# DLRM tower: one-hot lookups in steps of 512 columns over two alternating groups of five tables, in place of steps of 256 columns for a pair of tables

## The reference

```python
e = jnp.stack([tbl_f[ids[:, f]] for f in range(26)], axis=1)        # 2048 x 26 x 128
combined = jnp.concatenate([e, r_dense_x[:, None, :]], axis=1)      # 27 vectors a sample
z = jnp.einsum('bfd,bgd->bfg', combined, combined)[:, TRIU_I, TRIU_J]   # 351 pairs
h = jnp.concatenate([z, r_dense_x], axis=1)                         # 479
h = jnp.maximum(h @ W_top1 + b_top1, 0.0)                           # 512
h = jnp.maximum(h @ W_top2 + b_top2, 0.0)                           # 256
y = h @ W_top3                                                      # 2048 x 1
```

## Time and profile before

| | |
|---|---|
| three runs, us | 373.93 median, 371.11, 374.20 |
| profiled execution, us | 374.13 |
| its span, us | 371.9 |
| PE, PEld busy, us | 345.5, 317.1 |
| DVE, ACT, POOL busy, us | 170.1, 184.4, 258.8 |
| mean granted clock | 0.986 |
| moved by DMA | 37.14 MB, mean 100 GB/s |

### The profile page before, as it was taken

One profiled execution on the slowest core, in us unless ns is written; L12 is line 12 of the kernel. 1 busy time (PEld: TensorE's weight loads), 2 busy tenths in 40 slices (PEclk: granted clock), 3 DMA queues, 4 the chain that ended last, 5 costly groups with the idle time before them and its releaser, 6 DMA issues.

```text
span 371.9 us, 13580 instructions
## 1 busy us (share of the span) xinstructions
PE 345.5 (93%) x6176; PEld 317.1 (85%) x6176; DVE 170.1 (46%) x380; ACT 184.4 (50%) x235; POOL 258.8 (70%) x265
## 2 busy tenths in 40 slices
PE   1998787989998999999999999999999999999997
PEld 0898776879897889999899998999899998899887
DVE  4589654533533435356245535356244635350220
ACT  3588242764345543473716643473725734376433
POOL 6688877777777777777777777777777777774000
PEclk9999899999998999999999999999999999999999
DMA  7967743211622126221262226321262222221000
GB/s 242 356 183 243 232 149 107 67 51 51 196 70 67 51 58 183 78 65 51 68 198 53 65 54 173 91 67 53 51 206 60 64 53 65 55 56 37 19 4 3
DMA packets 15917, 37.14 MB, mean 100 GB/s; under 512 B 5141, under 2 KB 7829, under 8 KB 15860
## 3 DMA queue, kind: packets, MB, share of 16 engines
q0 software_dynamic: 8192, 16.79, 16.9%
q1 hardware_dynamic: 7668, 19.48, 16.1%
HBM read 36.24 MB, written 0.01 MB: 97 GB/s over the span
## 4 chain that ended last, share of the span: by engine, by line
PE 69%; POOL 20%; issue 7%; DMA 3%; SPq 0%; ACT 0%
PE ps_lk L509 29%; POOL rows L242 20%; PE ps_gram L536 10%; PE ps_tr L521 6%; PE ps_zt L562 6%; PE ps_mlp L562 6%; PE ps_mlp L569 3%; PE ps_zt L569 3%; DMA zt<-in_tbl 2%; PE ps_mlp L577 1%; PE ps_lk L590 1%; PE ps_lk L489 1%; PE ps_zt L549 1%; DMA rows<-in_tbl,gather_ids 1%; PE ps_lk L597 0%
## 5 line engine op out<-in xcount | busy, mean ns | idle before, releaser
L242 POOL DMA_INDIRECT rows<-in_tbl,gather_ids x256 | 257.4, 1006 | 80.4 <-issue 76.2
L279 DVE TENSOR_SCALAR onehot<-ids_from 128x512 fp32r<-128x512 f32 x320 | 126.3, 446 | 94.1 <-PE ps_lk L509 68.7
L509 PE MATMUL ps_lk<-onehot,table 128*128 128x256 f32 x1248 | 163.3, 290 | 2.6 <-DVE onehot L279 2.0
L509 PEld LDWEIGHTS ps_lk<-onehot,table 128*128 128x128 f32 x1248 | 155.9, 196 | 4.3 <-issue 3.1
L360 ACT COPY xt<-ps_tr 128x512 f32<-128x512 f32 x64 | 77.0, 1203 | 93.0 <-PE ps_tr L521 91.2
L536 PEld LDWEIGHTS ps_gram<-xt 128*26 128x26 f32 x4096 | 44.1, 103 | 23.4 <-issue 20.7
L536 PE MATMUL ps_gram<-xt 128*26 128x26 f32 x4096 | 52.7, 192 | 9.8 <-issue 4.8
L350 ACT COPY xt<-ps_lk 128x512 f32<-128x512 f32 x40 | 48.9, 1236 | 14.5 <-PE ps_gram L536 10.5
L287 DVE STREAM_TRANSPOSE zs<-ps_gram 128x832 f32<-128x832 f32 x16 | 16.8, 1050 | 85.9 <-PE ps_gram L536 85.9
L521 PE MATMUL ps_tr<-ident,rows 128*128 128x128 f32 x256 | 39.3, 276 | 3.3 <-ACT xt L360 1.8
L521 PEld LDWEIGHTS ps_tr<-ident,rows 128*128 128x128 f32 x256 | 29.6, 140 | 7.1 <-ACT xt L360 2.4
(11 more groups left out here) (57 smaller groups left out, 153.7 us busy)
## 6 DMA issues: line engine op xcount, KB each, us to landing
ids<-in_ids_onehot SPq DMA_DIRECT2D x8, 768.0 KB
w<-in_tbl SPq DMA_DIRECT2D x8, 512.0 KB, 5.0
rows<-in_tbl,gather_ids POOLq DMA_INDIRECT x256
ids<-in_ids_onehot SPq DMA_DIRECT2D x7, 512.0 KB
dense_x<-in_dense SPq DMA_DIRECT2D x8, 128.0 KB
zt<-in_dense SPq DMA_DIRECT2D x8, 128.0 KB
ids<-in_ids_onehot SPq DMA_DIRECT2D x2, 256.0 KB, 4.1
h<-in_tbl SPq DMA_DIRECT2D x1, 512.0 KB, 5.9
```

The source lines that it names most:

```text
L242: pool.indirect_dma_start(rows[n % ROW_BUFS][:, r, :], None, t_[f"tbl_{GATHERED[r]}"], bass.IndirectOffsetOnAxis(ap=gather_ids[:, n, r:r + ...
L279: nc.vector.tensor_scalar(onehot[:, u % RING, :, :], ids_from[:, 2 * i:2 * i + 2, :], float(k), None, ALU.is_equal).then_inc(s_unit, 1)
L509: m = nc.tensor.matmul(bank(c, i)[:, j, :], table[:, 2 * i + j, part, k, :], onehot[:, u % RING, j, :], start=(k == 0 and j == 0 and part ...
```

## The change

- **Steps.** A list `STEPS` of (first chunk, tiles, tables) takes the place of the pairs. From chunk 1 on the ten tables are two fives, `FIRST` (0 to 4) and `SECOND` (5 to 9). A wide step does one table for four tiles: 8 slices x 2 parts = 16 products of 512 columns. Chunks 1, 3 and 5 start wide steps of `FIRST` for themselves and the next chunk, chunks 2, 4 and 6 of `SECOND`. Narrow steps (one or two tables for one chunk) remain: six in chunk 0, three of `SECOND` in chunk 1, three of `FIRST` in chunk 7. That is 42 steps for 40, 30 of them wide.
- **First step.** `lookup_first` does table 0 alone in full floats: 8 products for 16.
- **Planes.** DVE compares the raw int32 ids with a per-partition scalar `own[:, k]`. ACT's shifts, `ids_from` and its waits are gone. Ids come by step, 512 columns to a buffer, four buffers.
- **Buffers.** `xt` holds four tiles instead of two; row buffers go from three to two; raw tables are staged in four buffers that rotate instead of three.
- **Order.** POOL's `LEAD` counts change; its rule from `b` = 5 on is the same. In chunk 1 PE does three more lookups before layer 1; in chunk 7 none is left. DVE makes the fourth step of chunk 1 and the following ones after `pack(1)`. The tail turns the last group of the last tile later, behind both halves of layer 2 of chunk 6 and half of layer 1 of tile 14, and does tile 14's layer 2 before tile 15's layer 1.

```diff
-CT = 2
-CHUNKS = TILES // CT
-CS = CT * P
...
+CT = 2
+CS = CT * P
+CHUNKS = TILES // CT
+XT = 2 * CT
+N = XT * P
+HALF = NO // 2
+FIRST, SECOND = list(range(HALF)), list(range(HALF, NO))
+def by_chunk(tables, first):
+    cuts = [tables[:first]] + [tables[i:i + 2] for i in range(first, len(tables), 2)]
+    return [tuple(b) for b in cuts if b]
+STEPS = []
+STEP0 = []
+for c in range(CHUNKS):
+    STEP0.append(len(STEPS))
+    if c == 0:
+        STEPS += [(c, CT, b) for b in by_chunk(FIRST + SECOND, 1)]
+    elif c == CHUNKS - 1:
+        STEPS += [(c, CT, b) for b in by_chunk(FIRST, 0)]
+    else:
+        STEPS += [(c, XT, (i,)) for i in (FIRST if c % 2 else SECOND)]
+        if c == 1:
+            STEPS += [(c, CT, b) for b in by_chunk(SECOND, 0)]
+STEP0.append(len(STEPS))
+assert CHUNKS % 2 == 0 and TILES % XT == 0
...
-ROW_BUFS = 3
+ROW_BUFS = 2
...
+IDS = 4
-LEAD = (0, 2, 8, 14, 20)
-SPLIT = list(range(2, NO)) + [0, 1]
+LEAD = (0, 2, 6, 12, 20)
+SPLIT = list(range(1, NO)) + [0]
...
+        xt = sb("xt", [P, N, NF])
+        ids = [sb(f"ids{b}", [P, N], I32) for b in range(IDS)]
+        onehot = sb("onehot", [P, RING, N], F32R)
+        own_i = sb("own_i", [P, KT], I32)
+        own = sb("own", [P, KT])
...
+        RAWS = len(stage) - 1
+        raw = [stage[0] if j == 0 else stage[1 + SPLIT.index(j) % RAWS] for j in range(NO)]
+        ps_lk = [pb(f"ps_lk{i}", [P, N]) for i in range(LB)]
+        ps_tr = pb("ps_tr", [P, GROUP * P])
...
+        def slot(n):
+            a = n % XT * P
+            return slice(a, a + P)
...
+            def load_ids(e):
+                if e >= IDS:
+                    sp.wait_ge(s_unit, (e - IDS + 1) * KT)
                     sp.sem_inc(s_carrier["sp"], 1)
+                sp.dma_start(ids[e % IDS][:, :], t_["ids_onehot"][e:e + 1, :].to_broadcast([P, N])
+                             ).then_inc(s_ids[e % IDS], 16)
...
             def load_raw(j):
+                n = SPLIT.index(j)
+                if j > 0 and n >= RAWS:
+                    sp.wait_ge(s_low, n - RAWS + 1)
...
+            load_ids(0)
+            load_raw(0)
+            load_raw(1)
+            load_raw(2)
+            load_ids(1)
+            load_raw(3)
+            load_raw(4)
+            load_ids(2)
+            load_ids(3)
+            load_ids(4)
+            load_raw(5)
+            load_raw(6)
+            load_ids(5)
+            load_raw(7)
+            load_raw(8)
             load_dense_x(0)
+            load_ids(6)
+            load_raw(9)
             sp.dma_start(cols[:, :], t_["cols"]).then_inc(s_cols, 16)
+            for e in range(7, 10):
+                load_ids(e)
             sp.wait_ge(s_low, NO)
+            sp.sem_inc(s_carrier["sp"], 1)
             load_dense_z(0)
             load_dense_x(1)
+            for e in range(10, STEP0[2]):
+                load_ids(e)
...
+                    for e in range(STEP0[c + 1], STEP0[c + 2]):
+                        load_ids(e)
...
-                        pool.wait_ge(s_gpart, max(b - 2 * PARTS, 0) + 1)
+                        pool.wait_ge(s_gpart, b - 2 * PARTS + 1)
...
+            def make_units(e):
+                dve.wait_ge(s_ids[e % IDS], (e // IDS + 1) * 16)
+                for k in range(KT):
+                    if k % USE == 0 and e > 0:
+                        dve.wait_ge(s_unit_used, ((e - 1) * KT + k) // USE + 1)
+                    w = STEPS[e][1] * P * len(STEPS[e][2])
+                    nc.vector.tensor_scalar(onehot[:, k, 0:w], ids[e % IDS][:, 0:w], own[:, k:k + 1], None, ALU.is_equal
+                                            ).then_inc(s_unit, 1)
...
+            make_units(0)
+            for e in range(1, STEP0[1]):
+                for n in range(len(STEPS[e][2])):
+                    low(STEPS[e][2][n] - 1)
+                make_units(e)
             low(NO - 1)
             dve.wait_ge(s_const, 3)
+            dve.sem_inc(s_carrier["dve"], 1)
+            make_units(STEP0[1])
+            pack(0)
+            make_units(STEP0[1] + 1)
+            make_units(STEP0[1] + 2)
+            pack(1)
+            for i in range(3, 7):
+                make_units(STEP0[1] + i)
             for c in range(1, CHUNKS - 1):
+                make_units(STEP0[c + 1] - 1)
+                make_units(STEP0[c + 1])
+                make_units(STEP0[c + 1] + 1)
+                pack(c * CT)
+                make_units(STEP0[c + 1] + 2)
+                if c + 2 < CHUNKS:
+                    make_units(STEP0[c + 1] + 3)
+                pack(c * CT + 1)
+            pack(TILES - 2)
+            pack(TILES - 1)
...
+            def evac(e):
+                _, w, tables = STEPS[e]
+                a, f = NG + 1 + tables[0], len(tables)
+                act.wait_ge(s_unit_used, (e + 1) * KT // USE)
+                if w == XT:
+                    nc.scalar.copy(xt[:, :, a], ps_lk[e % LB][:, :]).then_inc(s_lk, 1)
+                else:
+                    s = slot(STEPS[e][0] * CT).start
+                    nc.scalar.copy(xt[:, s:s + CS, a:a + f].rearrange("p s f -> p f s"),
+                                   ps_lk[e % LB][:, 0:f * CS].rearrange("p (f s) -> p f s", f=f)).then_inc(s_lk, 1)
...
                 if c == 1:
+                    evac_group(a, 2)
+                    for i in range(5, 8):
+                        evac(e + i)
...
+            c, a = CHUNKS - 1, TILES - 2
+            evac_group(a + 1, 0)
+            relu1(c - 1, 1)
+            evac_group(a + 1, 1)
+            relu1(c - 1, 2)
+            relu1(c - 1, 3)
+            evac_group(a + 1, 2)
+            relu2(c - 1, 0)
+            relu2(c - 1, 1)
+            evac_zt(a)
             keep_y(c - 1)
             last_relu1(0, 0)
             last_relu1(0, 1)
+            evac_group(a + 1, 3)
             last_relu1(0, 2)
             last_relu1(0, 3)
+            evac_zt(a + 1)
+            for j in range(T2):
+                last_relu2(0, j)
             for j in range(T1):
                 last_relu1(1, j)
+            for j in range(T2):
+                last_relu2(1, j)
...
+                pe.wait_ge(s_raw[0], 16)
                 for k in range(KT):
                     pe.wait_ge(s_unit, k + 1)
+                    m = nc.tensor.matmul(ps_lk[0][:, 0:CS], raw[0][:, k, :], onehot[:, k, 0:CS].bitcast(F32),
+                                         start=(k == 0), stop=(k == KT - 1))
                     if k % USE == USE - 1:
                         m.then_inc(s_unit_used, 1)
+            def lookup(e):
+                c, w, tables = STEPS[e]
+                if e >= LB:
+                    pe.wait_ge(s_lk, e - LB + 1)
+                if c == 0:
+                    pe.wait_ge(s_low, tables[-1])
+                elif e == STEP0[1]:
+                    pe.wait_ge(s_low, NO)
                 for k in range(KT):
                     if c == 0:
+                        pe.wait_ge(s_unit, e * KT + k + 1)
                     elif k % (KT // 2) == 0:
+                        pe.wait_ge(s_unit, e * KT + k + KT // 2)
+                    for j, i in enumerate(tables):
+                        x = slice(j * w * P, (j + 1) * w * P)
                         for part in range(2):
+                            m = nc.tensor.matmul(ps_lk[e % LB][:, x], table[:, i, part, k, :], onehot[:, k, x],
+                                                 start=(k == 0 and j == 0 and part == 0),
                                                  stop=(k == KT - 1 and part == 1), skip_group_check=True)
                     if k % USE == USE - 1:
                         m.then_inc(s_unit_used, 1)
...
+            turn(0, 0)
+            lookup(1)
+            lookup(2)
+            turn(0, 1)
+            lookup(3)
+            turn(0, 2)
+            lookup(4)
+            turn(0, 3)
+            lookup(5)
+            e = STEP0[1]
+            gram(0, 0)
+            lookup(e)
+            gram(0, 1)
+            turn(1, 0)
+            turn(1, 1)
+            lookup(e + 1)
+            turn(1, 2)
+            lookup(e + 2)
+            turn(1, 3)
+            gram(1, 0)
+            gram(1, 1)
+            for c in range(1, CHUNKS - 1):
+                a, e, f = c * CT, STEP0[c], STEP0[c + 1]
+                turn_pairs(a - 2)
                 if c == 1:
+                    turn(a, 0)
                 else:
+                    turn(a, 3)
                     layer3(c - 2)
+                lookup(e + 3)
+                turn_pairs(a - 1)
                 if c == 1:
+                    turn(a, 1)
+                lookup(e + 4)
                 if c == 1:
+                    turn(a, 2)
+                    for i in range(5, 8):
+                        lookup(e + i)
                     pe.wait_ge(s_cols, 16)
                     pe.wait_ge(s_w, 16 * 4)
                 layer1(c - 1, 0)
                 if c == 1:
+                    turn(a, 3)
+                gram(a, 0)
+                lookup(f)
+                turn(a + 1, 0)
                 layer1(c - 1, 1)
```

(42 more changed lines are left out.)

400 lines of the change are left out of this document (123 added, 277 removed).

## The result

| | before | after |
|---|---|---|
| timed runs on one chip, us | 374.06 median (371.11 to 376.16, 4 runs) | 389.56 median (384.58 to 392.34, 4 runs) |
| profiled execution, us | 374.13 | 387.75 |
| its span, us | 371.9 | 386.0 |
| mean granted clock | 0.986 | 0.951 |

The ratio is 1.0329, 95% interval 1.019 to 1.0469. The loss is clear of noise; whether it is over 2% is not, since the interval starts at 1.019. I had forecast 366.5 in a range of 361.5 to 377: the median lies 12.6 us above the range. The span of the profiled execution grew by 14.1 us, and that is what has to be found.

What follows compares the result with a forecast made beforehand. PE and POOL were taken to bound it side by side, PE slower by 1 us a chunk. PE's chunk 7 start of 325.5 plus its end gave span 364.3; 2.2 more made 366.5 us, range 361.5 to 377.

Steps and rivals of the forecast that it cites:

- Planes: VectorE: an int32 plane with a per-partition scalar costs 0.36 us as today, within 0.36 to about 0.64.
- POOL's wait: Chunk 0: POOL's one wait shrinks from 1.85 to 0.30 us, so every gather behind it comes 1.55 us earlier.
- the two causes that I gave it: Chunk 0: halved first step and no wait for ScalarE's id shift let VectorE start some 2 us sooner.
- Wide lookups: PE: a step of 16 products of 512 columns takes 3.6 us, saving 0.32 us on each of 27 steps.
- rival 1: Wide lookups on PE: width pays nothing, 238 ns a product, 375 us in all; chance 0.14.
- The bulge: Chunk 1 on PE: 80 narrow products for tables 5 to 9 ahead of its first gram, 9.8 us more.
- POOL's hold: Gather 65 waits for chunk 1's first gram half, at 91.7; POOL held about 0.6 us (0 to 5).
- Chunk 7: PE's last chunk: starts at 325.5, loses both its lookups, 2 x 3.92 us, and ends the span at 364.3.
- lower end: Range's 361.5 us: products at 216 ns, 27 x 0.1 less, PE then level with POOL.
- rival 4: Wide products stream faster than 216 ns, so POOL alone paces the kernel, 364 us; chance 0.04.
- Rival 2: VectorE's planes run at half pace, 0.64 us, adding 16 us before gather 65, about 382 us; chance 0.11.
- rival 3: Chunk 1's extra narrow products and waits hold POOL longer, + 4 us, 370.5 us; chance 0.17.

Runs made afterwards that it cites:

- a_const0_3: Kernel after, with only chunk 0's planes compared with constants, from ids ScalarE shifts to floats; third run, chip 14: 490.83 us, 0.9849 of before.
- a_rest: Kernel after, with VectorE waiting in chunk 0 before each step's low parts until PE has used the last step's planes: 496.70 us, 0.9876 of before.
- a_const0_4: Kernel after, with only chunk 0's planes compared with constants, from ids ScalarE shifts to floats; fourth run, chip 14: 489.05 us, 0.9769 of before.
- b_pointer: Kernel before, with planes compared with a per-partition scalar holding k instead of the constant k: 512.75 us, 1.0174 of before, chip 3.
- b_dense: Kernel before, with unused spare VectorE work behind packs of chunks 2 to 5 and 128 lookup products at the end: 516.68 us, chip 8.
- a_const0: Kernel after, with only chunk 0's planes compared with constants, from ids ScalarE shifts to floats; first run, chip 8: 483.86 us, 0.9838 of before.

## Why the prediction was wrong

Its sum was made on PE; here are its terms, in PE's time. Against the forecast chunk 0 lost 7.9 us, chunk 1 3.2, chunks 2 to 6 came out 0.2 better, and chunk 7 lost 10.7: together the 21.7 us between 364.3 and 386.0. Two steps failed, the planes' price and chunk 7.

- **Planes ("I take 0.36: same bytes, same layout").** This is the first step that failed. The row is 0.41 (3.25/8), the scalar is what costs it, and int32 is free. On VectorE that would still be small. What I had no term for is what these planes do to *another engine*: with no pauses around them they stretch GpSimd's gathers from 1.14 to 2.60 us in the mean. I predicted 1.55 us earlier for every gather, so 13.6 for the 9th and 25.2 for the 17th. POOL's wait did go, but gathers 7 and 8 already took 1.31 and 1.70 us: the 9th came at 14.46, and the 17th at 37.66. Chunk 0 was 7.9 us longer on PE instead of level.
- **Why VectorE has no pauses.** An earlier and unbroken VectorE was booked as a gain. Of the two causes that I gave it, freeing VectorE from ScalarE's shift is not needed: a_const0_3 has the shifts back and no pause either. That leaves the halved first step and the new order; no run takes them apart.
- **Wide lookups.** Forecast 3.6 a step, measured 3.75: the 216 ns pass of full floats was the wrong neighbour, and 234 ns lies close to my upper bound of 238, which is rival 1. The saving is 0.17 a step instead of 0.32, half the size, and 27 steps fall short by 4 us. That chunks 2 to 6 gained the forecast 10.5 all the same is the luck told above.
- **The bulge.** 9.8 forecast, 9.68 measured. The forecast for chunk 1 was 8.2 us above before, measured 11.4: 2.40 of waiting for planes behind the pack (I allowed about 2 in all), and 2.47 more because that lookup took 6.22 instead of 3.75.
- **POOL's hold.** 0.6 forecast for gather 65, 1.73 measured, but at 103.94 instead of 91.7: both chains were late together. After 54 us PE never waits for rows again. That POOL issues more slowly in the steady part too, 10.46 us a half tile for 10.31 (gathers 65 to 256), costs nothing here.
- **Chunk 7.** Forecast 38.8, measured 49.5: the second step that failed, and the larger one. I subtracted two lookups' time from a chunk in which they were also the cover, and left the clock at 2.4 GHz. PE was busy 40.25 us, where before without its two lookups it would have 33.3 (41.10 - 7.84); 9.25 us are idle, for 2.9 before. Most of the 7 us more of busy time is known products running long: 1.9 at 342.03, 1.0 at 369.98, and 0.9 for each group of the tail's layer 2 (1.92 for 1.06).
- **The range.** Its lower end doesn't follow: 27 x 0.1 less than 366.5 is 363.8, and even rival 4 ends at 364.

Rival 2, slower planes, was nearest in its sign and in its place ahead of gather 65, and wrong in how: it wanted 0.5 us a plane and PE waiting for them. Of PE's waits only 2.4 us in the middle of the kernel are for planes; the rest of the price went through GpSimd. Rival 1 happened nearly whole (234 of 238 ns), and rival 3 in part.

**Shown:** that the dense planes with the scalar delay the gathers (a_rest, a_const0_3 and a_const0_4, b_pointer, b_dense), that constants in chunk 0 are worth 2% on two chips whose grams pause, and that 234 ns is the product's own price. **Only argued:** that in the conditions of the first result the same repair gives back chunk 0's 7.9 us; no experiment ran in them. Even then some 382 us would remain, still slower than before: the rest is the bulge and chunk 7. For chunk 7 there is the trace, where the waits and the slow products stand; no run shows a gain in time from filling them. **Open:** what chunk 7 would take there with its lookups kept, and where the pauses of the gram products come from. The version to prefer so far is a_const0, where grams pause: there it beats before by 1.5 to 2.9% and the changed kernel by about 2%.

## What to carry to other kernels

An operation that a change makes "no dearer" on its own engine may have a second price on another engine, as VectorE's planes had on GpSimd's gathers; look at the *duration* of that engine's instructions beside it, not only at its waits. A pause that is removed may have been what let the neighbour work: be wary of packing an engine that is off the critical path at the start, if gathers are what PE waits for there. A total that comes out right (chunks 2 to 6) proves no term of the sum. And work taken out of the last stage takes its cover with it: count the waits that it hid, and take the stage's durations at the lower clock as the far end of the range.
